# Attention weights times values in 64x64 blocks, with the empty quarters left out and two banks summed

## The reference

```
q, k, v = split(shift(x) @ wqkv); q, k = rotary(l2norm(q)), rotary(l2norm(k))
for each window of 128 queries:   keys and values = [window before, own window]
    sim  = 8 * q @ keys.T                      # 128 x 256
    mask = (i < j) | (i > j + 128) | (j == -1) # i, j: position of query and key
    out  = softmax(where(mask, -inf, sim)) @ values
x = x + out @ wo;  x = x + (a * gelu(g)) @ w2, with a, g = split(layernorm(shift(x)) @ w1)
```

## Time and profile before

| what | us |
|---|---|
| median of 3 runs (3281.27 to 3283.43) | 3281.3 |
| the profiled execution | 3285.55 |
| its span, first to last instruction | 3283.7 |
| TensorE busy in it | 3166.6 (96%) |
| VectorE busy | 2714.0 (83%) |
| GpSimd busy | 2563.2 (78%) |
| ScalarE busy | 2151.3 (66%) |

### The profile page before, as it was taken

The page is one execution under the profiler, slowest core; times in us unless marked ns, Lnnn a source line. Parts: engine busy times, 40 slices in busy tenths (PEclk is TensorE's granted clock), DMA queues, the critical chain, the costliest instruction groups (busy, mean ns, idle before and its releaser), DMA issues.

```text
span 3283.7 us, 84999 instructions
## 1 busy us (share of the span) xinstructions
PE 3166.6 (96%) x25436; PEld 2431.2 (74%) x25436; DVE 2714.0 (83%) x8373; ACT 2151.3 (66%) x5372; POOL 2563.2 (78%) x2892
## 2 busy tenths in 40 slices
PE   5999999789999999999999999999999999999998
PEld 3666666457777777777777777777777777777777
DVE  5999999677878777777777788888888888888885
ACT  3555555447767676767676766776767676767674
POOL 3888888677777777777777777888888888888884
PEclk8999999999999999999999999999999999999999
DMA  6211111100000000000000001111111111111111
GB/s 217 74 44 44 45 45 44 42 11 26 26 25 24 24 24 24 24 24 24 24 24 24 25 25 33 37 37 38 37 38 37 38 38 38 39 38 39 38 37 30
DMA packets 153074, 125.03 MB, mean 38 GB/s; under 512 B 22580, under 2 KB 149032, under 8 KB 152368
## 3 DMA queue, kind: packets, MB, share of 16 engines
q1 hardware_dynamic: 146352, 110.67, 11.1%
q10 hardware_dynamic: 6272, 8.93, 0.9%
HBM read 77.51 MB, written 42.02 MB: 36 GB/s over the span
## 4 chain that ended last, share of the span: by engine, by line
PE 78%; DVE 10%; issue 7%; POOL 2%; ACT 1%; DVEq 1%; DMA 0%; SPq 0%; ACTq 0%; POOLq 0%
PE bank L539 27%; PE bank L735 19%; PE bank L743 10%; PE bank L546 7%; PE bank L708 7%; PE bank L687 6%; DVE shared L1061 2%; DVE a_den L1050 1%; DVE z L1016 1%; DVE a_den L1048 1%; DVE a_moments L1005 1%; DVE a_moments L1081 1%; DVE shared L1042 1%; DVE gated L1076 1%; DVEq L363 0%
## 5 line engine op out<-in xcount | busy, mean ns | idle before, releaser
L735 PEld LDWEIGHTS bank<-zT,W 128*128 128x128 f32 x5632 | 667.1, 192 | 137.3 <-issue 134.9
L539 PE MATMUL bank<-WQKV,xT 128*128 128x512 f32 x1536 | 744.5, 607 | 5.6 <-DVE rotary_work L1115 4.4
L1302 POOL TENSOR_TENSOR rnorm<-clamped,HALF 128x8 f32<-128x8 f32 x256 | 420.4, 1642 | 413.0 <-DVE clamped L1132 406.5
L735 PE MATMUL bank<-zT,W 128*128 128x128 f32 x5632 | 671.0, 275 | 13.8 <-issue 11.8
L1315 POOL TENSOR_TENSOR shared<-shared,share_of 128x512 f32<-128x512 f32 x512 | 584.8, 1170 | 62.1 <-DVE shared L1167 62.1
L904 ACT ACTIVATE shared<-shared,negmax 128x256 f32<-128x256 f32 x1024 | 505.6, 495 | 26.4 <-DVE negmax L1151 24.6
L539 PEld LDWEIGHTS bank<-WQKV,xT 128*128 128x128 f32 x1536 | 263.6, 191 | 217.4 <-issue 214.5
L1129 DVE TENSOR_REDUCE sums<-rotary_work 128x8 f32<-128x512 f32 x256 | 175.6, 686 | 288.7 <-ACT rotary_work L874 284.4
L1167 DVE COPY_PREDICATED shared<-BEYOND,shared 128x256 f32<-128x256 int32 x512 | 404.3, 801 | 0.0
L1151 DVE CUSTOM_DVE_ANT_0 shared<-bank,MASK 128x256 f32<-128x256 f32 x1024 | 365.7, 420 | 0.3 <-issue 0.3
L1325 POOL TENSOR_TENSOR shared<-shared,IDENT 128x256 f32<-128x256 f32 x512 | 362.1, 728 | 0.0
(11 more groups left out here) (144 smaller groups left out, 6669.3 us busy)
## 6 DMA issues: line engine op xcount, KB each, us to landing
X<-xl_rows SPq DMA_DIRECT2D x128, 128.0 KB, 2.3
X<-in_x SPq DMA_DIRECT2D x64, 128.0 KB, 2.1
x_tiles<-ax SPq DMA_DIRECT2D x64, 128.0 KB, 1.7
xl_rows<-axl SPq DMA_DIRECT2D x64, 128.0 KB, 1.7
XS<-xl_rows SPq DMA_DIRECT2D x128, 64.0 KB, 2.4
xm_rows<-X SPq DMA_DIRECT2D x128, 64.0 KB, 1.6
xs<-xm_rows SPq DMA_DIRECT2D x128, 64.0 KB, 1.8
xl_rows<-X SPq DMA_DIRECT2D x64, 128.0 KB, 1.7
```

Source lines behind the costliest of these rows:

```text
L539: mm = nc.tensor.matmul(held(tile, key)[:, 0:cols], lhsT[c], rhs[c], start=(c == 0), stop=(c == len(lhsT) - 1))
L735: mm = nc.tensor.matmul(held(tile, key)[:, k * P:(k + 1) * P], W1[:, tile.l, c, at:at + P], zT[:, c], start=(c == 0), stop=(c == KC - 1))
L1302: G.tensor_tensor(rnorm[q][:], clamped[q][:], HALF[:].to_broadcast((P, LH)), ALU.pow).then_inc(done[f"root_{key}"], 1)
```

## The change

Weigh becomes two steps (weigh0, weigh1: four heads each) of quarter-array products. Products with low keys (rows 0 to 63) go to bank `o`, those with high keys (rows 64 to 127) to a second bank `oo`. The two all-zero 64x64 blocks are skipped, so the remaining half of each of them is a product of 64 columns. The first product of each step is not split: it takes all 128 keys of the own window for one head (`every`), into `o`. That makes 30 products for a tile: 2 with 128 rows, 14 quarters of 128 columns and 14 of 64 columns.

The banks are summed in two steps: ScalarE copies `oo` to `oT` (`keep_oo`), then VectorE adds `o` to it (`keep_o`, new on VectorE, one slot later).

The lists are reordered. TensorE: after score come project_v, project_q, turn_k, weigh1, weigh0, widen2. ScalarE: square_q moves into the tile's own slot, after exp1; exp2 moves behind keep_k; exp3 moves one slot later, to the second place. VectorE: sum_q and rotate_q move to the end of the tile's own slot, behind invert0; invert1 to invert3 move one slot later, to the front, with keep_o behind them. GpSimd: root_q moves to the end of the tile's own slot, scale_q to the front of the next, and share1 and share2 move one slot later. All banks of phase L are handed out anew. Phase A and SyncE's list stay. The signals of weigh2 and weigh3 go and that of keep_oo comes; hunks that only rename such signals are left out below.

```diff
@@ -64,16 +64,15 @@
     "SP": [(0, "load"), (3, "shift"), (3, "late"), (5, "store")],
     "PE": [(5, "widen0"), (5, "widen1"), (3, "project_o"), (2, "turn_p1"), (0, "turn_x"), (2, "turn_p0"), (1, "turn_q"),
            (0, "project_k"), (5, "narrow"), (4, "turn_z_first"), (1, "ready_score"), (4, "turn_z_last"), (1, "score"),
-           (2, "weigh0"), (2, "weigh1"), (2, "weigh2"), (2, "weigh3"), (0, "project_v"), (4, "widen2"), (0, "turn_k"),
-           (0, "project_q")],
-    "ACT": [(1, "square_q"), (0, "age_k"), (4, "norm"), (5, "gelu"), (0, "keep_x"), (1, "keep_q"), (0, "square_k"),
-           (4, "affine"), (1, "exp0"), (1, "exp1"), (1, "exp2"), (1, "exp3"), (0, "keep_k"), (0, "keep_v"), (2, "keep_o")],
-    "DVE": [(1, "sum_q"), (1, "rotate_q"), (5, "gate0"), (5, "gate1"), (3, "add_o"), (5, "gate2"), (2, "keep_p0"),
-           (2, "keep_p1"), (0, "sum_k"), (0, "rotate_k"), (3, "stats"), (5, "add_f"), (1, "max0"), (1, "max1"), (1, "max2"),
-           (1, "max3"), (1, "invert0"), (1, "invert1"), (1, "invert2"), (1, "invert3")],
-    "POOL": [(2, "share3"), (2, "diagonal0"), (1, "root_q"), (1, "scale_q"), (2, "diagonal1"), (2, "diagonal2"),
+           (0, "project_v"), (0, "project_q"), (0, "turn_k"), (2, "weigh1"), (2, "weigh0"), (4, "widen2")],
+    "ACT": [(0, "age_k"), (2, "exp3"), (4, "norm"), (5, "gelu"), (0, "keep_x"), (1, "keep_q"), (0, "square_k"), (4, "affine"),
+           (1, "exp0"), (1, "exp1"), (0, "square_q"), (0, "keep_k"), (1, "exp2"), (0, "keep_v"), (2, "keep_oo")],
+    "DVE": [(2, "invert1"), (2, "invert2"), (2, "invert3"), (3, "keep_o"), (5, "gate0"), (5, "gate1"), (3, "add_o"),
+           (5, "gate2"), (2, "keep_p0"), (2, "keep_p1"), (0, "sum_k"), (0, "rotate_k"), (3, "stats"), (5, "add_f"),
+           (1, "max0"), (1, "max1"), (1, "max2"), (1, "max3"), (1, "invert0"), (0, "sum_q"), (0, "rotate_q")],
+    "POOL": [(1, "scale_q"), (2, "share1"), (2, "share2"), (2, "share3"), (2, "diagonal0"), (2, "diagonal1"), (2, "diagonal2"),
            (2, "diagonal3"), (4, "add_b2"), (0, "root_k"), (0, "add_k"), (0, "scale_k"), (3, "root_x"), (5, "finish"),
-           (1, "share0"), (1, "share1"), (1, "share2")],
+           (1, "share0"), (0, "root_q")],
 }
...
@@ -84,10 +83,10 @@
     "cum": "16375224",
 }
 BANK_L = {
-    "ag0": "47404747", "ag1": "30616215", "wo": "06215253", "p1": "62153030", "x": "47474747", "p0": "06215353",
-    "qT": "21530626", "k": "74747474", "nw": "30606215", "z": "62151530", "sim0": "15306212", "sim1": "74747474",
-    "sim2": "21530626", "sim3": "30621535", "o": "62153430", "v": "74747475", "ag2": "62171530", "kT": "06215306",
-    "q": "21530623",
+    "ag0": "57606240", "ag1": "40515762", "wo": "11111211", "p1": "33333333", "x": "40576240", "p0": "62405757",
+    "qT": "24057626", "k": "76240576", "nw": "40505762", "z": "11111111", "sim0": "40576242", "sim1": "05762404",
+    "sim2": "24057626", "sim3": "76240575", "v": "33333333", "q": "76240576", "kT": "11111111", "oo": "76240505",
+    "o": "05762424", "ag2": "62474057",
 }
 
 FILLS = {"a_turn_z": ["az"], "a_project": ["aqk"], "a_project_v": ["av"], "a_cum": ["cum", "kphi"], "a_turn_q": ["aq"],
...
@@ -124,8 +123,8 @@
     return min((d, k, step) for k, (d, step) in enumerate(order) if step in steps)[2]
 
 
-WEIGH = [f"weigh{p}" for p in range(PAIRS)]
-FILLS[earliest(ORDER_L["PE"], WEIGH)] = ["o"]
+WEIGH = ["weigh0", "weigh1"]
+FILLS[earliest(ORDER_L["PE"], WEIGH)] = ["o", "oo"]
 
 
 def banks_before():
...
@@ -694,20 +693,36 @@
                     after(pe, done[f"share{p}"], tile)
                 turn(tile, f"p{g}", [pr[p][:, 2 * k + 1] for p in (2 * g, 2 * g + 1) for k in range(2)]).then_inc(filled[f"p{g}"], 1)
 
-            def weigh(p, tile):
-
-
-                g = p // 2
-                first = f"weigh{p}" == earliest(ORDER_L["PE"], WEIGH)
+            def weigh(g, tile):
+
+
+                first = f"weigh{g}" == earliest(ORDER_L["PE"], WEIGH)
                 if first:
                     claim(pe, tile, "o")
+                    claim(pe, tile, "oo")
+                after(pe, done["keep_v"], tile)
                 after(pe, done[f"keep_p{g}"], tile)
-                after(pe, done["keep_v"], tile)
-                for kb, (slot, pT) in enumerate(zip(ages(tile), (pTold, pTnew))):
-                    for k, h in enumerate(heads_of(p)):
-                        mm = nc.tensor.matmul(held(tile, "o")[k * LD:(k + 1) * LD, p * P:(p + 1) * P], vring[tile.seq][:, slot, h * LD:(h + 1) * LD],
-                                              pT[g][:, 2 * (p % 2) + k], start=(first and kb == 0), stop=(kb == 1), skip_group_check=True)
-                mm.then_inc(done[f"weigh{p}"], 1)
+                older, newer = ages(tile)
+                low, high, every = slice(0, LD), slice(LD, P), slice(0, P)
+
+                def part(key, rows, slot, probs, p, k, queries, start, stop):
+                    h = heads_of(p)[k]
+                    return nc.tensor.matmul(held(tile, key)[k * LD:(k + 1) * LD, p * P + queries.start:p * P + queries.stop],
+                                            vring[tile.seq][rows, slot, h * LD:(h + 1) * LD], probs[g][rows, 2 * (p % 2) + k, queries],
+                                            start=start, stop=stop, skip_group_check=True)
+
+                for p in (2 * g, 2 * g + 1):
+                    opens = first and p == 2 * g
+                    for k in range(2):
+                        part("o", every if p == 2 * g and k == 0 else low, newer, pTnew, p, k, every, opens, False)
+                    for k in range(2):
+                        part("oo", high, older, pTold, p, k, every, opens, False)
+                    for k in range(2):
+                        part("o", low, older, pTold, p, k, low, False, True)
+                    for k in range(2):
+                        if p != 2 * g or k != 0:
+                            mm = part("oo", high, newer, pTnew, p, k, high, False, True)
+                mm.then_inc(done[f"weigh{g}"], 1)
 
             def project_o(tile):
                 after(pe, done["keep_o"], tile)
...
@@ -904,11 +919,11 @@
                     ins = nc.scalar.activation(rows, rows, ACT.Exp, scale=-1.0, bias=negmax[:, h:h + 1], accum_out=den[:, h:h + 1])
                 ins.then_inc(done[f"exp{b}"], 1)
 
-            def keep_o(tile):
+            def keep_oo(tile):
                 after(act, done[last_weigh], tile)
                 after(act, filled["wo"], tile, back=1)
                 first_use(act, tile)
-                copy(flat(oT), held(tile, "o")[:]).then_inc(done["keep_o"], 1)
+                copy(flat(oT), held(tile, "oo")[:]).then_inc(done["keep_oo"], 1)
 
             def norm(tile):
                 after(act, done["root_x"], tile, per=2)
...
@@ -1169,13 +1184,16 @@
             def keep_p(g, tile):
 
                 after(dve, filled[f"p{g}"], tile)
-                for p in (2 * g, 2 * g + 1):
-                    after(dve, done[f"weigh{p}"], tile, back=1)
+                after(dve, done[f"weigh{g}"], tile, back=1)
                 after(dve, done[f"diagonal{g}"], tile, per=2)
                 first_use(dve, tile)
                 got = held(tile, f"p{g}").rearrange("p (a t) -> p a t", a=4)
                 V.tensor_tensor(pTnew[g], got, CAUSAL[:].unsqueeze(1).to_broadcast((P, 4, P)), ALU.mult)
                 V.copy_predicated(pTold[g], as_bits(LATER, 4), got).then_inc(done[f"keep_p{g}"], 1)
+
+            def keep_o(tile):
+                after(dve, done["keep_oo"], tile)
+                V.tensor_tensor(oT.rearrange("p a t -> p (a t)"), held(tile, "o")[:], oT.rearrange("p a t -> p (a t)"), ALU.add).then_inc(done["keep_o"], 1)
 
             def add_o(tile):
                 after(dve, done["norm"], tile, back=1)
...
@@ -1317,8 +1335,7 @@
             def diagonal(b, tile):
 
                 after(pool, done[f"share{b}"], tile)
-                for p in (b // 2 * 2, b // 2 * 2 + 1):
-                    after(pool, done[f"weigh{p}"], tile, back=1)
+                after(pool, done[f"weigh{b // 2}"], tile, back=1)
                 first_use(pool, tile)
                 old = pr[b].rearrange("p (e b) t -> p e b t", e=2)[:, :, 0]
                 k = 2 * (b % 2)
```

More of the change, by code:

```diff
@@ L102 @@
               "sim0": "max0", "sim1": "max1", "sim2": "max2", "sim3": "max3", "p0": "keep_p0", "p1": "keep_p1",
-              "o": "keep_o", "wo": "add_o", "z": "affine", "ag0": "gate", "ag1": "gate",
+              "o": "keep_o", "oo": "keep_oo", "wo": "add_o", "z": "affine", "ag0": "gate", "ag1": "gate",
               "ag2": "gate", "nw": "add_f"}
@@ L112 @@
              "stats", "norm", "gate", "add_f", "add_k", "root_k", "scale_k", "root_q", "scale_q", "share0",
-             "share1", "share2", "share3", "root_x", "add_b2", "gated", "finish", "weigh0", "weigh1", "weigh2", "weigh3", "other_mask",
+             "share1", "share2", "share3", "root_x", "add_b2", "gated", "finish", "weigh0", "weigh1", "keep_oo", "other_mask",
```

(7 more changed lines are left out.)

1 line of the change is left out of this document (removed).

## The result

The changed kernel takes 3405.5 us (median of 4 runs, 3404.46 to 3410.54) against 3282.4 for the kernel before on the same chip: 1.0375 times as long, interval 1.0362 to 1.0388. That is slower, as forecast, but by 123 us, where 83 were forecast and 110 was the upper end of the range. The profiled execution took 3404.6 us, 119 more than the profiled one before.

What follows compares the result with a forecast made beforehand. TensorE's queue was taken to bound the kernel at 20.12 us a tile; +0.02 streaming and +0.64 shape changes, taken as 0.65, times 128 tiles gave 83 us more: 3364 us median (3369 profiled), range 3322 to 3392.

Steps and rivals of the forecast that it cites:

- the tile: TensorE's queue per tile: +0.02 us streaming and +0.64 changes of shape, taken as +0.65 on 20.12.
- Leaving score's side: Weigh no longer next to score on TensorE: one more excursion from full-array shape, +0.19 us a tile.
- weigh: Weigh's two blocks on TensorE between turn_k and widen2: 2.35 us in all.
- the openers: Two 128-row products opening weigh1 and weigh0: 0.44 us streaming and three inner shape changes at 0.15, 0.89 together.
- The opener's change: TensorE's shape change from 128x64 opener to 64x64 quarters: taken as 0.15 us each, between nothing and 0.20.
- keep_o in an even tile: VectorE's new sum ends before project_o is due: by over 1 us in the first layer, perhaps 0.2 in the second.
- the step that finds the other engines hidden: VectorE, ScalarE and GpSimd steps checked against TensorE's due times in a tile: all in time, adding nothing.
- the sum made from it: TensorE's extra 0.65 us a tile times 128 tiles: 83 us more, 3364 us median, 3369 profiled.
- the cover: VectorE's keep_o, ending at 22.9 to 24.2 us, stays hidden ahead of project_o, due at 24.35.
- Keep_o is late: Rival: slow inverts make project_o wait 0.1 to 0.3 us in one or both layers, 3370 to 3402; 12 in 100.
- The opener's free change: Rival: TensorE's change from opener to quarters costs nothing, +0.35 us a tile, 3326 us; 14 in 100.
- the openers' overlap with the quarters: Part of a rival in weigh, with inner shape changes free too: net -0.23 us a tile, 3252 us; 7 in 100.

Runs made afterwards that it cites:

- e10_before_flat_all: Kernel before, with layer loops of TensorE, VectorE, ScalarE and GpSimd replaced by their slots one after the other: 3267.0 us, 0.9949 of the kernel before.
- e11_quarters_flat_all: Changed kernel with openers split into quarters, keep_o first on VectorE's list, layer loops of TensorE, VectorE, ScalarE and GpSimd written out: 3244.1 us, 0.9877.
- e3_no_opener: Changed kernel with both opening products split into quarters, weigh's waits and claims moved ahead of turn_k: 3335.7 us, 1.0159 of the kernel before.

## Why the prediction was right and where it failed

**Right: the tile.** TensorE's queue bounds it; +0.67 a tile where the sum had +0.65. Leaving score's side measured 0.20 (0.19 forecast), weigh 2.37 (2.35), the openers 0.87 (0.89). The opener's change, which no row showed, is not free: the quarters start 0.15 us later than its streaming alone would have them. By the prediction's own terms the range runs from 3326 to 3393, not from 3322 to 3392; nothing hangs on it. The trace agrees with the rule that a change of mode, and not only of the tile, drains TensorE (the Trainium skill, TensorEngine Tiling (Array Packing), Key Properties), here even where only the rows change, and gives it the price of 0.14 to 0.20 us.

**Right: keep_o in an even tile.** It was forecast in time by more than 1 us in the first layer and perhaps 0.2 in the second; in the second it was in time by 1.1. The copies behind the inverts took 0.43 to 1.2 us and not 1.2 throughout.

**Failed: the step that finds the other engines hidden, and the sum made from it.** The prediction put VectorE's steps end to end at an even period, wrote of keep_o "If the cover goes, TensorE waits for the difference, nothing more", and multiplied one even tile by 128. Where the loops jump back, neither the even period nor the cover holds. The lists were moved past the seam: rotate_q on the one side and the inverts with keep_o on the other have VectorE's 5.5 us of standing between them, ahead of project_o, where before it lay in a wait for square_q. And TensorE's own seam moved from behind project_q, where 3.32 us of issued work cover the branch, to behind weigh and widen2, where 1.8 do. Neither has a term in the sum. The missing 33 us of the profiled execution are 12 x 2.8; the two layers measured 3.2 and 2.4. Of the 50 us that the changed kernel's jumps cost, TensorE's standing is 29 and the clock about 21 (1.9 us at the jump followed, eleven falls). The clock's share is in no row of before, whose layers have the clock at 1.00.

The evidence was among the rows quoted: "13.8 <-issue 11.8" in the earlier trace rows, twelve waits of up to 1.4 us, each at the seam. I read that row for its count of records alone.

**The rivals.** "Keep_o is late" named the right wait for a wrong reason, contention in every tile at 0.1 to 0.3 us; it showed as a wait of TensorE in the layers only when TensorE's jump was moved or taken away, at twelve places, of up to 3.7 us, and from another cause. The opener's free change and the openers' overlap with the quarters are refuted by weigh's 2.37 and 1.50 and by the opener's rows.

**Settled and open.** That both seams make the missing part is shown from both sides: one alone gives 2 or 5 us, both 35, all four 50, and with none the two kernels differ by 89, the even tiles' 86 and little more. Moving the seam by two steps in the kernel before costs 21 us by itself. How long TensorE stands is the branch's time, plus 0.5, less the work issued ahead of it. Open is why the branch takes longer in some kernels and layers (3.3 to 6.0 us), and when the clock falls. That the instructions of the lap's start arrive late is my reading of the jump. It is not shown, but rows speak for it. Two DMA queues carry packets of the kind "instruction": in the changed kernel 9 to 11 start in a tile with a jump, 2.6 on average in another. With TensorE written out a tile with a jump has 8.2 on average, with VectorE 7.0, with both 5.2, and with all four (e10_before_flat_all, e11_quarters_flat_all) no tile has more than 5.

## What to carry to other kernels

An even tile times the number of tiles is a sum for even tiles only. Look for waits whose count is that of the loop's laps, see what covers each engine's jump back (how many microseconds its last records run), and before a list is reordered ask which two steps will face each other across the seam and who waits for the second. A wide product put among packed ones costs two changes of shape besides its own time.

## What the runs showed of the hardware

- TensorE, VectorE and ScalarE each stand at their own jump, and not equally long: TensorE stood 0.6 to 2.9 us in these two kernels, VectorE up to 5.8, ScalarE up to 1.9 before and 3.3 after. TensorE's branch itself lasts 3.4 to 4.1 us, and 15 to 17 records issued ahead of it run meanwhile. Writing all four out saved 50 us in the changed kernel, 4.1 for each of twelve jumps, and 18 in the one before, 1.5 for each.
- After 2.22 us of standing, the clock fell to the 1.2 GHz level a microsecond after TensorE had resumed, and came back some 3 us later. The jumps of the kernel before, up to 1.4 us, had no such fall. Nor had one jump of the changed kernel, the longest on its chain (2.87 us at 2314.16: scores at 2304.73 and 2328.67, 3.15 us over an even tile, granted clock 1.00 behind it), nor three of e3_no_opener (2.98, 3.36 and 3.38 us). The length of the pause alone does not decide, and what does stays open.
- Four lanes of 64x64 products run side by side with 64- and 128-column records mixed: 64 records in 1.50 us, against 1.90 for the 32 half-array records of the same sums.
- A result that comes 0.3 us ahead of its product instead of 1.1 costs that product 0.19 us, with no wait shown on the chain.
